# A ViT tower in one kernel: the feed-forward's inner activations turned by DMA and converted on VectorE, instead of turned by TensorE and read on ScalarE

## The reference, cut to what matters

```python
h = tok(x)                                   # patches x weights, 64 images
h = concat([cls_tok, h])                     # (64, 197, 192)
h = h + attn(layernorm(h))                   # 12 heads of 64, 4-bit fake quantisation
h = h + ffn(layernorm(h))

def bitlinear(x, w, g):                      # used twice in ffn
    x_norm = x * rsqrt(mean(x * x) + 1e-6) * g
    scale = 127.0 / max(max(abs(x_norm)), 1e-5)          # one for each row
    x_q = clip(round(x_norm * scale), -128, 127) / scale
    return x_q @ ternary(w).T
def ffn(x):                                  # D = 192, H = 512
    up, gate = split(bitlinear(x, w_in, g_in), 2)        # 2 x 512 columns
    return bitlinear(silu(gate) * up, w_out, g_out)      # back to 192 columns
```

## Time and profile before

| | us |
|---|---|
| median of three runs (lowest, highest) | 1308.37 (1306.78, 1312.17) |
| the profiled execution, its own time | 1312.79 |
| its span, first to last instruction | 1310.6 |
| engine busy over the span: PE / DVE / ACT / POOL | 1129.8 / 1084.5 / 937.1 / 475.0 |
| mean granted TensorE clock over the span | 0.899 |
| feed-forward stage, from `tin`'s first load | 946 to 1310.6 |
| first and last `y` operation | 963.00 and 1299.73 |

### The profile page before, as it was taken

One profiled execution on the slowest core, in us unless ns is written; L12 is line 12 of the kernel. 1 busy time (PEld: TensorE's weight loads), 2 busy tenths in 40 slices (PEclk: granted clock), 3 DMA queues, 4 the chain that ended last, 5 costly groups with the idle time before them and its releaser, 6 DMA issues.

```text
span 1310.6 us, 31925 instructions
## 1 busy us (share of the span) xinstructions
PE 1129.8 (86%) x10782; PEld 696.3 (53%) x10782; DVE 1084.5 (83%) x1978; ACT 937.1 (71%) x1877; POOL 475.0 (36%) x540
## 2 busy tenths in 40 slices
PE   4999996599999999999999999998457677767776
PEld 4999995145555555555555555554334344434443
DVE  4566778179999999999999999999478888989995
ACT  0000000599999999999999999997168888888886
POOL 7444444002222222222222222222256666666664
PEclk9999998799999999999999999999557876777776
DMA  6999995136555556555555566555312322332322
GB/s 242 297 286 292 288 302 178 43 123 148 146 150 147 141 139 137 137 148 147 150 145 141 138 137 140 146 145 147 68 50 80 88 85 80 88 90 84 89 69 76
DMA packets 157637, 187.62 MB, mean 143 GB/s; under 512 B 42784, under 2 KB 119664, under 8 KB 157168
## 3 DMA queue, kind: packets, MB, share of 16 engines
q1 hardware_dynamic: 86352, 136.71, 32.7%
q10 hardware_dynamic: 55808, 39.65, 9.9%
q0 software_dynamic: 15360, 9.70, 8.5%
HBM read 143.06 MB, written 36.12 MB: 137 GB/s over the span
## 4 chain that ended last, share of the span: by engine, by line
PE 70%; ACT 8%; DVE 6%; issue 6%; ACTq 4%; DMA 3%; POOL 2%; SPq 0%; DVEq 0%; POOLq 0%
PE psum L1088 18%; PE psum L1148 11%; PE psum L1031 11%; PE psum L1135 8%; PE psum L1118 7%; PE psum L1179 6%; PE psum L1101 5%; ACT yi L579 2%; ACTq L449 2%; DMA big<-xt 2%; ACT big L572 2%; ACT ysq L599 2%; DVE big L1006 1%; ACT zi L587 1%; PE psum L1200 1%
## 5 line engine op out<-in xcount | busy, mean ns | idle before, releaser
L674 POOL DMA_DIRECT2D h_res<-att x128 | 143.4, 1169 | 574.3 <-ACT att L517 565.2
L883 DVE TENSOR_TENSOR pi<-big 128x2364 int16<-128x2364 f32 (+1 forms) x128 | 334.7, 2615 | 3.4 <-DMA big<-z_row 3.2
L541 ACT ACTIVATE big<-psum 128x788 f32<-128x788 f32 (+1 forms) x384 | 317.0, 828 | 1.2 <-DVE pi L883 1.2
L1031 PE MATMUL psum<-big 128*128 128x192 f32 (+1 forms) x1200 | 196.8, 329 | 18.4 <-DMA big<-xt 18.4
L1031 PEld LDWEIGHTS psum<-big 128*128 128x128 f32 (+1 forms) x1200 | 194.8, 190 | 19.5 <-DVE big L719 17.0
L1088 PE MATMUL psum<-xT,w1b 128*128 128x394 bf16 x768 | 163.9, 337 | 27.4 <-DMA xT<-x_int 25.2
L1179 PE MATMUL psum<-winb,zT 96*128 96x512 bf16 (+1 forms) x396 | 151.1, 551 | 33.2 <-DVE big L1006 32.3
L503 ACT ACTIVATE qki<-psum 128x394 int16<-128x394 f32 x384 | 172.3, 512 | 4.8 <-PE psum L1088 3.8
L503 ACT ACT_TABLE_LOAD x1 | 1.3, 1283 | 239.7 <-issue 239.7
L1148 PE MATMUL psum<-big,sa_hot 128*32 128x197 f32 (+1 forms) x3072 | 168.2, 336 | 0.0
L708 POOL TENSOR_TENSOR big<-big,goutb 128x512 f32<-128x512 f32 (+1 forms) x99 | 123.7, 1270 | 81.6 <-DVE big L1006 81.6
(11 more groups left out here) (100 smaller groups left out, 1699.5 us busy)
## 6 DMA issues: line engine op xcount, KB each, us to landing
big<-z_row SPq DMA_DIRECT2D x192, 394.0 KB, 5.0
big<-xt SPq DMA_DIRECT2D x98, 384.0 KB, 4.4
tin<-h_res SPq DMA_DIRECT2D x49, 192.0 KB, 2.4
tres<-h_res ACTq DMA_DIRECT2D x49, 192.0 KB, 2.5
out<-oo ACTq DMA_DIRECT2D x49, 192.0 KB, 2.6
h_res<-big ACTq DMA_DIRECT2D x96, 96.0 KB, 3.8
x_int<-big ACTq DMA_DIRECT2D x96, 64.0 KB, 3.8
h_res<-att POOLq DMA_DIRECT2D x64, 96.0 KB, 3.4
```

The source lines that it names most:

```text
L541: act.activation(ex[0:r, tri, t, 4 * g:4 * g + 4, :].rearrange("p (a h) n -> p a h n", a=2), psum[0:r, 2 * t:2 * t + 2, 0:2 * N] .rearrang ...
L674: pool.dma_start(h_res[bass.ds(b - 4, 1), t0:t0 + r, :].rearrange("a n d -> (a n) d"), att[0:r, par, t, :], accum_op=ALU.add).then_inc(s_a ...
L883: v.tensor_tensor(pi[0:r, t, :, 0:N], ex[0:r, it, t, :, :], zb[0:r, ip, :, :], ALU.mult).then_inc(s_pi, 1)
L1031: last = mm(psum[p0:p0 + r, s, 0:D], xring[:, s, c * 128 + p0:c * 128 + p0 + r], weight_of(cls, c), start=(c == 0), stop=(c == KC - 1))
```

## The change

1. PE's eight transposes of `yi` and ACT's read of them are removed. In their place SP issues one transposing DMA for each pair, from `yi3` into a new int16 buffer `yTi` (256 KB for a whole pair, 8 blocks of 128 x 128), and DVE converts it to bf16 `yT3` with one `tensor_copy` of 128 x 1024 (a `CAST` in the rows).
2. The output matmuls, `oo`, the load of `tres` and the store come one pair later (`pair(6)`, `pair(6)`, `pair(5)`, `pair(7)`). On PE the output matmuls now stand at the head of a step, ahead of the `w_in` matmuls. On DVE the new copy stands behind the reduction of `yg`, and `oo` stands ahead of `y`.
3. The dequantising factors get a ring of four in a tensor `ft`, so their operation stands among the other factor operations, ahead of `y`, and no longer waits for `y`.
4. SP loads `tin` one step earlier in its own stream, ahead of the transposing DMA.

```diff
@@ SP, pair_step
+                if at := pair(-1):
+                    wait_apart(sp, s_t["zc"], t)
+                    sp.dma_start(tin[0:r, oth, 0:n, :], pair_rows(h_att, t + 1, r, n)).then_inc(s_t3[oth], 16)
+                if at := pair(4):
+                    wait_apart(sp, s_t["yi"], t - 3)
+                    wait_apart(sp, s_t["yT_read"], t - 5)
+                    sp.dma_start_transpose(yTi[:, par, 0:4 * n, 0:r], yi3[0:r, par, 0:n, :].rearrange("p a h -> p (a h)"))\
+                      .then_inc(s_ym[par], 16)
@@ ACT, pair_step
-                if at := pair(5):
-                    act.wait_ge(s_t["yT_summed"], t - 4)
-                    act.activation(yT3[:, 0:n, :, 0:r], psum[:, 5, :].bitcast(i16)
-                                   .rearrange("p (a c n) -> p a c n", a=2, c=4)[:, 0:n, :, 0:r], ACT.Copy)\
-                       .then_inc(s_t["yT_read"], 1)
...
-                    wait(act, s_t["yT_summed"], t - 5)
+                    if not isinstance(t, int) or t > 5:
+                        act.wait_ge(s_ym[par], loads_of(t - 6, par))
@@ DVE, pair_step, behind the reduction of yg
+                if at := pair(6):
+                    dve.wait_ge(s_ym[par], loads_of(t - 6, par))
+                    wait(dve, s_t["o_summed"], t - 6)
+                    v.tensor_copy(yT3[:, 0:n, :, 0:r], yTi[:, par, 0:4 * n, 0:r]
+                                  .rearrange("p (a c) n -> p a c n", c=4)).then_inc(s_t["yT_read"], 1)
...
                 factors(2)
+                factors(4)
...
                 factors(3)
+                if at := pair(6):
+                    dve.wait_ge(s_t["o_summed"], t - 5)
...
+                        ins = v.scalar_tensor_tensor(oo[0:r, par, a, :], psum[0:r, 6, a * D:(a + 1) * D],
+                                                     ft[0:r, (q + 2) % 4, 1, a:a + 1], tres[0:r, par, a, :],
+                                                     ALU.mult, ALU.add)
...
-                if at := pair(3):
-                    dve.wait_ge(s_t["y"], 2 * (t - 3) + at[1])
-                factors(4)
-                if at := pair(5):
-                    dve.wait_ge(s_t["o_summed"], t - 4)
...
@@ PE, pair_step
+                if at := pair(6):
+                    pe.wait_ge(s_t["yT_read"], t - 5)
+                    wait(pe, s_t["o_ready"], t - 6)
+                    for a in range(n):
+                        for c in range(4):
+                            last = mm(psum[0:r, 6, a * D:(a + 1) * D], yT3[:, a, c, 0:r], woutb[:, c, :],
+                                      start=(c == 0), stop=(c == 3))
+                    last.then_inc(s_t["o_summed"], 1)
                 if at := pair(3):
                     pe.wait_ge(s_t["xT_read"], t - 2)
...
-                if at := pair(5):
-                    pe.wait_ge(s_t["yi"], t - 4)
-                    wait(pe, s_t["yT_read"], t - 5)
-                    dst = psum[:, 5, :].bitcast(bf16).rearrange("p (a c n) -> p a c n", a=2, c=4)
-                    for a in range(n):
-                        for c in range(4):
-                            last = nc.tensor.transpose(dst[:, a, c, 0:r], yi3[0:r, oth, a, c * 128:(c + 1) * 128].bitcast(bf16),
-                                                       ident[0:r, 0:r])
-                    last.then_inc(s_t["yT_summed"], 1)
-                if at := pair(5):
-                    pe.wait_ge(s_t["yT_read"], t - 4)
...
```

More of the change, by code:

```diff
@@ L181, in vit_tower_kernel @@
             "xT_summed", "xT_read", "hid", "silu", "y", "square", "yg", "y_amax", "yms", "y_rms",
-            "yi", "yT_summed", "yT_read", "o_summed", "o_ready")}
+            "yi", "yT_read", "o_summed", "o_ready")}
         s_t3 = [sem(f"ffn_in_{p}") for p in range(2)]
         s_t3b = [sem(f"ffn_residual_{p}") for p in range(2)]
+        s_ym = [sem(f"ffn_y_turned_{p}") for p in range(2)]
         s_sq0 = sem("ffn_first_square")
@@ L324, in vit_tower_kernel @@
         wdeq4 = sb("wdeq4", [128, 2, 2], fp32)
-        MS, RMS, MAX, T_, A127, INV, S_, F_ = range(8)
+        ft = sb("ft", [128, 4, 2, 2], fp32)
+        MS, RMS, MAX, T_, A127, INV, S_ = range(7)
         def val(which, par, k, rows, n=None):
@@ L342, in over_pairs @@
             for t in range(first):
-                step(t, t % 2)
+                step(t, t % 2, t % 4)
             whole = (NPAIR - 1 - first) // UNROLL * UNROLL
@@ L346, in over_pairs @@
                 for j in range(UNROLL):
-                    step(UNROLL * i + first + j, j % 2)
+                    step(UNROLL * i + first + j, j % 2, (first + j) % 4)
             for t in range(first + whole, NPAIR + LAGS):
-                step(t, t % 2)
+                step(t, t % 2, t % 4)
         def pair_rows(dram, j, rows, n):
@@ L607, in pair_step @@
                         ins.then_inc(s_t["square"], 1)
-                if pair(4) or pair(6):
-                    wait(act, s_t["o_ready"], min(t - 5, NPAIR) if isinstance(t, int) else t - 5)
-                if at := pair(4):
+                if pair(5) or pair(7):
+                    wait(act, s_t["o_ready"], min(t - 6, NPAIR) if isinstance(t, int) else t - 6)
+                if at := pair(5):
                     r, n = at
-                    act.dma_start(tres[0:r, par, 0:n, :], pair_rows(h_att, t - 4, r, n)).then_inc(s_t3b[par], 16)
-                if at := pair(6):
+                    act.dma_start(tres[0:r, oth, 0:n, :], pair_rows(h_att, t - 5, r, n)).then_inc(s_t3b[oth], 16)
+                if at := pair(7):
                     r, n = at
-                    act.dma_start(pair_rows(out, t - 6, r, n), oo[0:r, par, 0:n, :]).then_inc(s_t3o[par], 16)
+                    act.dma_start(pair_rows(out, t - 7, r, n), oo[0:r, oth, 0:n, :]).then_inc(s_t3o[oth], 16)
             for p in range(2):
@@ L1168, in _, with pair_step @@
             pe.wait_ge(evac["y"], B)
-            def pair_step(t, par):
+            def pair_step(t, par, q):
                 pair, oth = pair_of(t), 1 - par
+                if at := pair(6):
+                    r, n = at
+                    pe.wait_ge(s_t["yT_read"], t - 5)
+                    wait(pe, s_t["o_ready"], t - 6)
+                    for a in range(n):
+                        for c in range(4):
+                            last = mm(psum[0:r, 6, a * D:(a + 1) * D], yT3[:, a, c, 0:r], woutb[:, c, :],
+                                      start=(c == 0), stop=(c == 3))
+                    last.then_inc(s_t["o_summed"], 1)
                 if at := pair(3):
```

49 lines of the change are left out of this document (19 added, 30 removed).

## The result

The changed kernel takes 1509.62 us (median of four runs, 1508.61 to 1510.4) against 1308.26 before. The ratio is 1.1533, 95% interval 1.1507 to 1.1559: slower by 15%. The prediction was 1515, range 1415 to 1550.

The account below looks back on a forecast made before the run. Before, DVE nearly set the 6.89 us step; after, a y-to-y line across engines sets 11.25. 47 x (11.25 - 6.89) = +205, +2 tail, on 1312.8 gives 1520, or 1515 in terms of the median; range 1415 to 1550.

Parts of the forecast that it names:

- The line: From y to y through POOL, DVE, PE and ACT, work runs in sequence: 11.67 us slow, 9.16 fast; main case chance 0.60.
- The terms: Pieces from y to y, through reduction, copy, PE's matmuls and transposes, zT's read and SiLU: sum 11.67 us at lower clock.
- the bounds: DVE's new int16 to bf16 copy: 0.52 us taken, with 0.37 and 0.56 kept as bounds.
- The clock: PE's bursts mostly at the lower clock, mean step 11.25 us; rival with PE often or always at upper clock, chance 0.18.
- the slow step: One step from y to y with PE wholly at the lower clock: 11.67 us.
- Savings beside the line: PE's transposes, ACT's 1.02 us read and 0.53 us of DVE's factors, taken off, only lengthen idle time.
- The transposing DMA: Rival on SP's new DMA: at 13.5 us each without overlap it bounds the step, total 1621 us; chance 0.08.
- the prediction's other estimate: For SP's transposing DMA of 256 KB, 1.0 us from the Trainium skill's 261 GB/s; by it the DMA rival falls.
- The copy held by POOL: Rival on DVE: POOL's whole 0.69 us root holds up the copy, +32 us more, total 1547; chance 0.06.
- The signs: Profile marks: PE waits about 6 us a step for the copy, reduction 1.2 for POOL, y 3 to 4 for SiLU.
- The other side: Rival: the y-to-y line stays open and DVE bounds a 6.1 us step, 37 us won, total 1271; chance 0.03.

Follow-up runs that it names:

- the first experiment: Changed kernel with PE's output matmuls moved back behind the w_in matmuls and the transposes of zi: 1332.16 us, ratio 1.0178 to the kernel before.
- the run with the copy first: Changed kernel with DVE's copy moved from behind the reduction of yg to the head of the step: 1398.33 us, ratio 1.0673 to the kernel before.
- the fillers: Changed kernel plus 12 unused matmuls of 512 columns at the end of each PE step: 1485.54 us, ratio 1.1354 to the kernel before.
- the orders of PE and DVE put right: Changed kernel with output matmuls last on PE and oo behind y on DVE: 1299.07 us, ratio 0.9922 to the kernel before.
- two more edits: On the 1299.07 us kernel, reduction of yg cut in two and ACT reordered to squares, zi, yi: 1274.55 us; on the kernel before with factors ahead: 1307.68.
- 1292.39 us: The 1299.07 us kernel with ACT reordered to squares, zi, yi and the reduction whole: ratio 0.9866 to the kernel before.
- 1298.7 us: The 1299.07 us kernel with only the reduction of yg cut in two, tile 0 ahead of the statistics: ratio 0.9918 to the kernel before.

## Why the prediction was right

- **The line closes through PE's order.** Shown by the first experiment: moving the output matmuls gives back 177 us. For this line the prediction's list of what is queued behind which wait was complete. That the copy's place behind the reduction puts POOL's product on the line is shown by the run with the copy first, which gives back 111.
- **The terms.** At the lower clock 11.67 predicted and 11.59 measured in one step. Predicted for measured: `y` to reduction 3.36 for 3.44, the reduction's share 1.14 for 1.14, copy and passage 0.57 for 0.47, output matmuls 1.24 for 1.26, `w_in` and transposes 4.01 for 4.04, zT to SiLU 0.59 for 0.50, SiLU to `y` 0.71 for 0.70.
- **The copy**: 0.52 guessed on the line between two other forms, 0.42 measured, inside the bounds. Predicted for 47 steps was +205 and measured +195.2, 0.2 us a step less; the copy's 0.1 us makes 5 of these 10 us. Part of the closeness of 1515 to 1509.62 is luck: the forecast took 4.4 us off for the profiled execution of before, which lay that far above the median, and the changed kernel's profiled execution lay only 0.3 above its own, so that shift hides some 4 of the 10 us.
- **The clock.** I took 0.4 us off the slow step for bursts that end fast, and the mean step is 0.54 under the slow one read above. Stage mean 0.61, "below 0.65" predicted. So not every burst is slow: a step of 11.59 throughout would have made the 47 steps 26 us longer. That the clock is on the line was shown by the fillers; how much of it one can win back I had oversized: I expected 9.2 to 10.2 us and the step was 10.36, since the clock fell within the `w_in` matmuls, behind PE's remaining wait of 3.3 us.
- **Savings beside the line.** For the factors' 0.53 us it is shown that they bring nothing by themselves, on the kernel before, ratio 1.0003. For PE's transposes of `yi` and ACT's read no run shows it alone. ACT's read stood between zT's read and the SiLU, and both of these are on the line, so to count its 1.02 us as beside the line was wrong; the sum is right all the same, since it has the SiLU directly behind zT's read.
- **The transposing DMA** was no rival: landing in 3.1 us, where scaling by size said 6 to 18. Attention's landings were no measure for it, and the prediction's other estimate, 1.0 us, was too short by 2.1 but right about the rival.
- **The copy held by POOL** didn't come in the changed kernel. It starts at 1213.76, POOL's root at 1213.46, and it still takes 0.42, and none of the 50 takes over 0.44, so the root doesn't block it. Begun beside POOL's product the copy is held up, as the copy-first run shows.
- **A wait that I didn't list**: `oo` for the store, 23.7 us in 36 steps. By the timeline it cost nothing, since `oo` ends at 1217.23 and `y` waits for the SiLU until 1220.77; I had not followed the store when its place moved.
- **The signs.** PE's wait for the copy came as written (301.7 us in all, 6.0 a time). Two waits were off in size: the reduction waits 1.5 us for POOL where 1.2 was written, and `y` 2.9 for the SiLU where 3 to 4 was written (means of the rows above).
- **The other side** (the route pays if the line stays open) existed after all, in other kernels: 0.9922 with the orders of PE and DVE put right, and 0.9727 with two more edits that win nearly nothing on the old route. But an open line alone didn't give the 6.1 us a step and 1271 us that the prediction wrote for it: the step was 6.58, with DVE waiting for POOL's product, and 6.09 came only with both further edits.

Not tried: another order of ACT or PE on the old route that would keep the transposes off the line, and a rule for how many fillers PE needs at which place to keep the clock up in the `w_in` matmuls.

## What to carry to other kernels

Before costing a moved operation, list all that is queued behind it on its engine and ask who waits for those; a consumer at the head of a step ties everything behind it to its producer's place in the step. Engines that each have time to spare can still take turns, and then the step is the sum of their turns. A busy share of 88% doesn't tell that an engine sets the time: take work off it in a separate run and see whether a wait takes the place. Where two waits end together, edits that each gain nothing may gain together.

## What the runs showed of the hardware

- A conversion of int16 to bf16 of 128 x 1024 on VectorE takes 0.42 us alone or beside GpSimd's root, and 1.06 (median of 50) when begun during GpSimd's products of 128 x 512.
- While the copy and the root overlap, it is the root that can be longer. In two steps of the changed kernel's timeline:

```profile
1202.97 0.42 DVE L992 CAST big<-big 128x1024 bf16<-128x1024 int16 x1
1202.99 0.94 POOL L695 TENSOR_TENSOR pt<-pt,neg_half 128x2 f32<-128x2 f32 x1
...
1213.46 0.75 POOL L695 TENSOR_TENSOR pt<-pt,neg_half 128x2 f32<-128x2 f32 x1
```

Begun just behind the copy the root takes 0.94 us, begun 0.30 ahead of it 0.75, and 0.69 with no copy beside it. Over all steps it takes 0.74 in the median and 0.96 at most here, and 0.69 and 0.70 in the kernel with the copy first.

- A transposing DMA of 256 KB from SBUF to SBUF lands in 3.1 us (median), less than the 5.5 of one of 104 KB from DRAM in the attention stage, where other transfers run beside it.
- The `tin` load lands in 3.4 us in the changed kernel for 2.4 before, and the store in 3.5 for 2.6 (medians). The transposing DMA alone isn't the reason: the kernels of 1274.55 and 1292.39 us have it in every step, and there the two land in 2.4 and 2.5. What goes with the slow landings is that the `tin` load is issued within 0.5 us of the load of `tres` and of the store: at 1202.27, with the others at 1201.83 and 1202.30, in the changed kernel, but at 1201.00, with 1202.92 and 1203.49, in the kernel of 1274.55 us. In the four other kernels with `tin` as close to both (1332.16, 1299.07, 1398.33 and 1298.7 us) it lands in 3.4 to 3.5. No run moves one transfer alone, so the cause is not shown.
